# Rows scattered by expert and running rank in attention, and a second mixture that starts on full blocks inside the end of attention

## The chip, the cores and the metric

One NeuronCore of a Trainium2 chip runs the whole program. The metric is the device time of one execution in microseconds, as a median of several runs. Beside it one execution is recorded by the hardware profiler; all rows shown are of that one.

## The reference

Sixteen sequences of 256 tokens, 256 wide (N = 4096 tokens). What matters here is the last layer; the stages before it are a first mixture of experts, a product-key layer (its stage is called the peer stage) and a recurrence.

```
h = layernorm(x); q, k, v = h @ w_qkv + b_qkv
x = x + softmax(q k^T / 4) v @ w_o + b_o                    # 16 heads
h = layernorm(x) * ln2_g + ln2_b
topv, topi = top_k(h @ gate_w + gate_b, 2); gw = softmax(topv)   # 8 experts
out_e = relu(h @ W1[e] + b1[e]) @ W2[e] + b2[e]             # 256 -> 1024 -> 256
return x + sum over the two chosen e of gw * out_e
```

## The kernel before

Five engines (TensorE, VectorE, ScalarE, GpSimd, SyncE) each run a list of instructions in the order in which the code writes them, and meet through semaphores. Nothing is reordered: an instruction that waits holds all behind it on its engine. `e.wait_ge(s["x"], n)` is such a wait.

**Peer stage.** 32 blocks of 128 tokens. SyncE stores x1 (`x1_sync`), writes the recurrence's input to a scratch in HBM and reads it back (`xw_sync`); it has nothing else to do there.

**Attention.** `attn_tensor`, `attn_vector`, `attn_scalar`, `attn_gpsimd` and `attn_sync` walk over slots t; a sequence q starts every four slots, and `at(t, o)` gives the q whose step of offset o falls in slot t. A unit i (64 in all, four a sequence) is eight heads' halves: `rows_tensor` (scores for the maxima), `cols_tensor` (transposed scores), `exp_scalar`, `values_tensor`. By sequence there are, in this order: `xh_gpsimd` (slot 4q-2: the normed rows, line 1430), `h1_tensor` (slot 4q, line 1441), projections, the maxima (`max_sync`, whose rows go by DMA), `back_tensor`/`back_vector` (transposing the heads back and dividing), `oT`, `wo_tensor` (L1636), `res_vector` (the residual, L1645), `norm2_vector` (statistics and a first guess of 1/sigma), `norm2_gpsimd` (adds x to the output buffer, L1675; twelve small Newton operations, L1380 to L1386; `norm2_end`, L1668), `h2_tensor`, `gate_tensor` (L1703) and `gate_vector` (L1709), `top_vector` (two best experts), `weight_scalar`/`weight_vector`, and `rows_store_sync`, which stores the normed rows and their two weights at the token's place in `xn_scratch`. The loop ends with slot 66; the tail (units 58 to 63, sequences 13 to 15) is written out by hand.

**Routing.** When all sequences are through, `route_vector` and `route_tensor` count the 8192 choices per expert by matmuls with a triangle and with ones, give each choice a slot in blocks of 128 of one expert, and invert that table (which token stands in slot s) with one-hot tables and 64 f16 matmuls (`invert_vector`, `invert_tensor`, line 181). All engines then meet in `stage_end`.

**Second mixture.** NBK = 71 blocks of 128 slots, enough for any split. GpSimd gathers a block's rows by an indirect DMA (`xs_load_gpsimd`, helper line 206) and adds the block's result to the output by another that accumulates (`y_add_gpsimd`, L2387). TensorE runs, for n = 0 to 71: `head_tensor(n+1)` (two transposes), `up_tensor(n)` (32 matmuls, L2253), `down_tensor(n-1)` (16 matmuls, L2268). VectorE copies the expert's W1 (`w1_vector`, L2326, 128x2048) and evacuates half of the hidden units, ScalarE copies W2 and evacuates the other half. The PSUM banks alternate between two blocks.

## Time and profile before

| | |
|---|---|
| median of 3 runs | 2958.82 us (2957.26 to 2960.76) |
| the profiled execution | 2952.11 us |
| its span, first to last recorded instruction | 2950.3 us |
| mean granted TensorE clock | 0.987 of full |
| first mixture and peer stage | up to some 1976 us |
| attention | to 2396 us |
| routing | 2396 to 2421 us |
| second mixture | 2421 to 2950 us |

PE is TensorE's matmuls, PEld its weight loads, DVE VectorE, ACT ScalarE, POOL GpSimd, SP SyncE (SPq its DMA issues). L12 is line 12 of the kernel; the line can be that of a helper, so gathers of all stages show as L206. A bracket at a row's end is the idle time before it and what ended it.

### The profile page before, as it was taken

The numbers are of one execution on the slowest core, as the hardware profiler recorded it, in microseconds if no ns is written. First come the engines' busy times: TensorE is split into PE (matmuls) and PEld (weight loads), VectorE is DVE, ScalarE is ACT, GpSimd is POOL, SyncE is SP. The second block draws the span as 40 slices with busy tenths as digits, with TensorE's granted clock in tenths as the row PEclk, the third lists the DMA queues.
The fourth block names the chain that finished last, engine by engine and source line by source line (L and its number), as shares of the span: only waits on it lengthen the run. The fifth ranks groups of instructions, "written<-read, shape, count | busy, mean of one in ns | idle before, by whom it ended". The sixth has DMA issues, their size and how long they took to land.

```text
span 2950.3 us, 72654 instructions
## 1 busy us (share of the span) xinstructions
PE 2836.3 (96%) x28558; PEld 2186.6 (74%) x28558; DVE 1917.1 (65%) x6569; ACT 1213.0 (41%) x2720; POOL 496.9 (17%) x642
## 2 busy tenths in 40 slices
PE   8999879999999999999999999988999969999998
PEld 4795468777777777777777777655666659999998
DVE  4563487777777777777777777556777754444443
ACT  2332232433333333333343433245555535555554
POOL 0554400000000000000000000022444323333333
PEclk9999989999999999999999999999999979999999
DMA  3552400101010101010101010111222142222222
GB/s 142 170 164 79 148 1 23 34 23 34 24 34 23 34 23 34 23 34 23 34 23 34 23 34 23 43 46 41 70 77 63 49 133 35 39 37 37 37 37 33
DMA packets 94322, 148.90 MB, mean 50 GB/s; under 512 B 20048, under 2 KB 76240, under 8 KB 90896
## 3 DMA queue, kind: packets, MB, share of 16 engines
q1 hardware_dynamic: 73728, 107.83, 11.1%
q0 software_dynamic: 20112, 36.40, 6.1%
q8 instruction: 228, 3.74, 0.5%
q14 instruction: 110, 0.90, 0.1%
q10 hardware_dynamic: 144, 0.03, 0.0%
HBM read 95.93 MB, written 48.27 MB: 49 GB/s over the span
## 4 chain that ended last, share of the span: by engine, by line
PE 86%; DVE 5%; DMA 4%; ACT 2%; issue 2%; SPq 0%; POOL 0%; POOLq 0%; DVEq 0%; ACTq 0%
PE ps L1008 16%; PE ps L827 15%; PE ps L2253 9%; PE ps L1077 8%; PE ps L2268 8%; PE ps L1044 4%; PE ps L989 4%; DMA arena<-ys_scratch,arena 3%; PE ps L420 2%; PE ps L431 2%; PE ps L857 2%; PE ps L858 2%; PE ps L1564 2%; PE ps L1515 1%; PE ps L1585 1%
## 5 line engine op out<-in xcount | busy, mean ns | idle before, releaser
L827 PEld LDWEIGHTS ps<-arena 128*128 128x128 f32 x4096 | 537.5, 193 | 29.0 <-issue 2.9
L1008 PE MATMUL ps<-arena 128*128 128x256 f32 x2048 | 549.8, 392 | 1.9 <-DVE arena L1018 1.0
L827 PE MATMUL ps<-arena 128*128 128x128 f32 x4096 | 540.0, 276 | 0.9 <-ACT arena L835 0.9
L1008 PEld LDWEIGHTS ps<-arena 128*128 128x128 f32 x2048 | 354.2, 190 | 162.9 <-issue 132.9
L835 ACT ACTIVATE arena<-ps 128x256 f32<-128x256 f32 x512 | 195.3, 382 | 543.2 <-PE ps L827 542.6
L1077 PE MATMUL ps<-arena 128*16 128x256 f32 x4096 | 270.6, 382 | 8.2 <-DVE arena L1107 7.4
L1805 POOL MEMSET arena<- 128x3072 f32 x1 | 2.7, 2657 | 1566.3 <-PE ps L1008 1566.3
L2253 PE MATMUL ps<-arena 128*128 128x128 f32 x2272 | 265.4, 275 | 0.0
L2253 PEld LDWEIGHTS ps<-arena 128*128 128x128 f32 x2272 | 259.4, 192 | 0.2
L2268 PE MATMUL ps<-arena 128*128 128x256 f32 x1136 | 256.8, 379 | 0.0
L1098 DVE SCALAR_TENSOR_TENSOR arena<-arena 128x128 f32<-128x128 f32 x256 | 73.8, 288 | 280.4 <-ACT arena L1089 280.4
L2268 PEld LDWEIGHTS ps<-arena 128*128 128x128 f32 x1136 | 210.5, 190 | 25.7
L1089 ACT ACTIVATE arena<-ps 128x256 f32<-128x256 f32 x256 | 98.1, 383 | 305.3 <-PE ps L1077 305.3
L1526 DVE TENSOR_REDUCE arena<-ps 128x2 f32<-128x512 f32 (+1 forms) x192 | 155.8, 863 | 50.8 <-PE ps L1515 50.6
L1077 PEld LDWEIGHTS ps<-arena 128*16 128x16 f32 x4096 | 94.5, 96 | 125.3 <-issue 63.4
L2354 DVE TENSOR_TENSOR arena<-ps,arena 128x256 f32<-128x256 f32 x71 | 30.1, 425 | 224.8 <-PE ps L2268 224.8
L2387 POOL DMA_INDIRECT out<-arena x71 | 114.6, 1614 | 316.5 <-DVE arena L2360 313.5
L972 DVE TENSOR_TENSOR arena<-arena 128x2048 f16<-128x2048 f16 x128 | 155.4, 1214 | 0.0
L998 DVE TENSOR_TENSOR arena<-arena,ps 128x1024 f32<-128x1024 f32 x128 | 151.6, 1184 | 0.0
L989 PE MATMUL ps<-arena 64*128 64x32 f16 x8192 | 123.9, 174 | 13.8 <-DVE arena L977 13.8
L2297 ACT ACTIVATE arena<-arena 128x2048 f32 x71 | 135.5, 1908 | 3.4 <-PE ps L2268 2.9
L989 PEld LDWEIGHTS ps<-arena 64*128 64x128 f16 x8192 | 111.3, 93 | 30.5 <-DVE arena L977 15.4
(288 smaller groups left out, 4626.7 us busy)
## 6 DMA issues: line engine op xcount, KB each, us to landing
xw_scratch<-arena SPq DMA_DIRECT2D x32, 512.0 KB, 2.7
arena<-xw_scratch SPq DMA_DIRECT2D x256, 64.0 KB, 2.7
arena<-in_W SPq DMA_DIRECT2D x16, 1024.0 KB, 5.3
ys_scratch<-arena SPq DMA_DIRECT2D x71, 128.0 KB
xn_scratch<-arena SPq DMA_DIRECT2D x32, 129.0 KB, 3.2
arena<-in_xT SPq DMA_DIRECT2D x8, 512.0 KB, 8.4
arena<-in_kinT SPq DMA_DIRECT2D x8, 512.0 KB
arena<-in_xtb SPq DMA_DIRECT2D x32, 128.0 KB, 2.3
```

What stands on the lines that cost most here:

```text
L827: m = e.matmul(bank(b)[:, 128 * i:128 * i + 128], kin[:, k, 2 * jp + i, :], xcT[:, k, 128 * blk:128 * blk + 128], start=(k == 0), stop=(k ...
L835: e.activation(G[blk % 2][:, 2 * jp:2 * jp + 2, :], bank(2 + jp % 2)[:, 0:256].rearrange("p (a b) -> p a b", a=2), ACT.Gelu).then_inc(s["G ...
L972: e.tensor_tensor(X[b], iota_pairs(128), pairs(r_[:, 0, t0:t0 + 16], 128), ALU.is_equal)
L989: m = e.matmul(bank(4 + half)[:, 32 * q:32 * q + 32], X[b][p0:p0 + 64, q // 2, :, q % 2], Y12[b][p0:p0 + 64, i, q // 2, :, q % 2], start=( ...
L998: e.tensor_tensor(gv, gv, bank(4, 2).rearrange("p (g t j) -> p g j t", g=2, j=32), ALU.mult).then_inc(s["A"], 1)
L1008: m = e.matmul(bank(7)[:, 0:256], G[blk % 2][:, j, :], kout[:, j, :], start=(j == 0), stop=(j == 31))
L1044: m = e.matmul(bank(h), xcT[:, k, 128 * blk:128 * blk + 128], Wx[:, k, 512 * h:512 * h + 512], start=(k == 0), stop=(k == 1))
L1077: m = e.matmul(gate_ps[32 * g:32 * g + 16], hT_, Wh[:, k, 256 * g:256 * g + 256], start=False, stop=(k == 1), skip_group_check=True)
L1526: e.tensor_reduce(mx[q % 2][:, :, c, 4 * v + j:4 * v + j + n].rearrange("p b j -> p j b"), bank(b + j, n).rearrange("p (j b k) -> p j b k" ...
L2253: m = e.matmul(bank(b)[:, 128 * (f % 4):128 * (f % 4) + 128], Wb1[i][:, k, 128 * f:128 * f + 128], hb[i][:, k], start=(k == 0), stop=(k == 1))
L2268: m = e.matmul(bank(6 + i)[:, 0:256], hid[i][:, f], Wb2[i][:, f], start=(f == 0), stop=(f == 7))
L2297: e.activation(Wb2[n % 2].rearrange("p a b -> p (a b)").unsqueeze(1), Wr2[:, bass.ds(r, 1)], ACT.Copy).then_inc(s["a_w2"], 1)
```

## The change

**Rows.** Each expert gets an area of PITCH = 4224 rows in `xn_scratch`, which now holds 1152 x 31 rows of 260 words: 256 values, two weights, the token's number and its first expert. In the peer stage SyncE fills all of it with pad rows, 1152 at a time. After each sequence's `top_vector`, `choice_vector` makes one-hot rows of the two choices; one period later `before_tensor` counts, with a triangle and ones in f16, the equal choices ahead of each token, and `rank_vector` adds the running count per expert and has four lists of 128 row numbers. `rows_out_gpsimd` writes the rows of the sequence there with four indirect DMAs, in place of SyncE's two plain ones. The inversion and the barrier are gone.

**Blocks.** After sequence 7, `first_table_vector` (slots 57 and 58) lists the blocks that are full by then; they serve for the first FIRST_N = 24 of the 71. `last_table_vector`, in three parts behind blocks 7 to 9, lists the rest. Both tables give an expert and 128 consecutive rows per block. NBK stays 71.

**Order.** The second mixture's blocks 0 to 4 are interleaved by hand with the end of attention for sequences 13 to 15, on all engines. Blocks below RAMP = 6 have one set of PSUM banks (4, 5, 6, 7), so that `head`, `up` and `down` of a block wait for their evacuations in the block before. Buffers move: the gathered rows lie on rows of `hall` that have been written out, `Wb1` and `Wb2` on keys, queries and values, `b2r` on `OT` (loaded after `back` of sequence 15). The norm of sequence 15 goes from VectorE to GpSimd. W1 and W2 are loaded at other slots.

```diff
@@ peer_sync
                 xw_sync(e, blk)
+                if blk < 31:
+                    e.dma_start(xnd[FILL * blk:FILL * blk + FILL], I["padrow"]).then_inc(s["nrow"], 16)
@@ new functions
+        def route_init_vector(e):
+            d = s["qd"]
+            e.tensor_scalar(run[0], iota8, float(PITCH), None, ALU.mult).then_inc(d, 1)
+            e.memset(c1, 0.0).then_inc(d, 1)
+            e.tensor_copy(tri16, tri).then_inc(d, 1)
+            e.tensor_copy(one16, ones).then_inc(d, 1)
+            e.wait_ge(s["nrow"], 528)
+            e.tensor_copy(hall_u[:, :, 258], ids).then_inc(d, 1)
+        def choice_vector(e, q):
...
+            e.tensor_copy(hall[:, m, 259], ii8[:, m, 0]).then_inc(d, 1)
+            e.tensor_copy(r_i.rearrange("p (a b) -> p a b", b=2), ii8[:, m, 0:2]).then_inc(d, 1)
...
+            e.tensor_tensor(r_o, r_i.unsqueeze(2).to_broadcast([128, 4, 8]), iota8.unsqueeze(1).to_broadcast([128, 4, 8]),
+                            ALU.is_equal).then_inc(d, 1)
...
+            e.tensor_tensor(r_s, o[:, :, 0], o[:, :, 1], ALU.add).then_inc(d, 1)
+        def before_tensor(e, q, b):
+            r = bank(b)
+            e.wait_ge(s["qd"], seq(q) + 4)
+            e.matmul(r[:, 16:32], tri16, flat(r_s), start=True, stop=False)
+            e.matmul(r[:, 24:32], one16, r_s[:, 0], start=False, stop=True)
+            e.matmul(r[:, 32:40], one16, r_s[:, 0], start=True, stop=False)
+            e.matmul(r[:, 32:40], one16, r_s[:, 1], start=False, stop=True).then_inc(s["as_cum"], 1)
+        def rank_vector(e, q, b):
...
+            e.tensor_copy(slots[:, 4 * q:4 * q + 4], r_f).then_inc(d, 1)
+        def rows_out_gpsimd(e, q):
+            if q:
+                e.wait_ge(s["rsc"], 64 * q)
+            e.wait_ge(s["po_xn"], q + 1)
             e.wait_ge(s["po_dd"], 4 * q + 4)
+            e.wait_ge(s["qd"], seq(q) + 9)
+            for j in range(2):
+                for k in range(2):
+                    c = 4 * q + 2 * j + k
+                    e.indirect_dma_start(xnd, bass.IndirectOffsetOnAxis(ap=slots[:, c:c + 1], axis=0), hall[:, 2 * q + j], None
+                                         ).then_inc(s["rsc"], 16)
@@ attn_tensor, attn_vector
                     gate_tensor(e, q)
+                    if q:
+                        before_tensor(e, q - 1, 6)
...
                 for q in at(t, 24):
                     gate_vector(e, q)
+                    if q:
+                        rank_vector(e, q - 1, 6)
...
                     top_vector(e, q)
+                    choice_vector(e, q)
+                if t in (57, 58):
+                    first_table_vector(e, t - 57)
@@ attn_gpsimd
                 for q in at(t, -2):
                     if q:
                         xh_gpsimd(e, q)
-            for q in (13, 14, 15):
-                norm2_gpsimd(e, q)
+                for q in at(t, 29):
+                    rows_out_gpsimd(e, q)
@@ moe2_tensor
             head_tensor(e, 0)
-            for n in range(NBK + 1):
+            e.wait_ge(s["ot"], 63)
+            values_tensor(e, 63, 0)
+            head_tensor(e, 1)
+            up_tensor(e, 0)
...
+            gate_tensor(e, 13, 3)
+            before_tensor(e, 12, 3)
...
+            back_tensor(e, 15, 0)
+            head_tensor(e, 2)
+            up_tensor(e, 1)
...
+            oT_tensor(e, 15, 2)
+            down_tensor(e, 0)
+            wo_tensor(e, 15, 0)
...
+            h2_tensor(e, 14, 1)
+            head_tensor(e, 3)
+            up_tensor(e, 2)
...
+            gate_tensor(e, 14, 3)
+            before_tensor(e, 13, 3)
+            down_tensor(e, 1)
...
+            h2_tensor(e, 15, 2)
+            head_tensor(e, 4)
+            up_tensor(e, 3)
...
+            for n in range(5, NBK + 1):
                 if n + 1 < NBK:
                     head_tensor(e, n + 1)
                 if n < NBK:
                     up_tensor(e, n)
-                if n:
-                    down_tensor(e, n - 1)
+                down_tensor(e, n - 1)
@@ moe2_gpsimd
-            e.wait_ge(s["iv"], 39)
-            for n in range(NX):
-                xs_load_gpsimd(e, n)
+            norm2_gpsimd(e, 13)
+            xs_load_gpsimd(e, 0)
+            xs_load_gpsimd(e, 1)
+            rows_out_gpsimd(e, 10)
+            rows_out_gpsimd(e, 11)
+            norm2_gpsimd(e, 14)
+            xs_load_gpsimd(e, 2)
+            xs_load_gpsimd(e, 3)
+            rows_out_gpsimd(e, 12)
             for n in range(NBK):
                 y_add_gpsimd(e, n)
                 if n + NX < NBK:
                     xs_load_gpsimd(e, n + NX)
+                if n == 0:
+                    norm2_gpsimd(e, 15)
+                if n < 3:
+                    rows_out_gpsimd(e, 13 + n)
@@ gate2_vector
+            if n >= NX:
+                e.wait_ge(s["acc"], 16 * (n - NX + 1))
```

## Rows read from the trace of the kernel before

**Rows 1.** The page, part 1: busy us (share of the span) and instructions

```profile
PE 2836.3 (96%) x28558; PEld 2186.6 (74%) x28558; DVE 1917.1 (65%) x6569; ACT 1213.0 (41%) x2720; POOL 496.9 (17%) x642
```

**Rows 2.** Windows: each engine's busy us, then granted clock, DMA share, GB/s

```profile
2396.00:2421.00 25.00, 9.54 (x69) 7.68 (x69) 21.88 (x60) 5.14 (x5) 0.00 (x0) 0.57 0.21 66
...
2421.00:2427.00 6.00, 5.28 (x19) 4.20 (x19) 2.89 (x6) 0.67 (x2) 4.53 (x4) 0.77 0.17 44
...
2460.00:2560.00 100.00, 100.00 (x695) 93.76 (x694) 47.62 (x140) 52.68 (x98) 36.11 (x28) 1.00 0.24 38
```

**Rows 3.** The chain that ended last, from 2377 to 2442 us: start, us, what

```profile
2377.07 1.07 PE ps L1585 x16
...
2417.81 1.23 PE ps L181 x16
...
2427.39 3.70 PE ps L2253 x32
...
2431.31 3.57 PE ps L2253 x32
...
2438.56 3.57 PE ps L2253 x32
```

**Rows 4.** The same chain at the span's end

```profile
2934.74 3.47 PE ps L2268 x16
```

**Rows 5.** Timeline, first gathers and last add: start, us, engine, line [idle before]

```profile
2421.56 1.66 POOL L206 DMA_INDIRECT arena<-xn_scratch,arena  x1 [33.84 <-DVEq L73]
...
2421.87 1.23 DVE L2326 COPY arena<-arena 128x2048 f32 x1 [1.09 <-issue]
...
2425.05 0.16 DVE L2345 TENSOR_TENSOR arena<-arena 128x1 f32<-128x1 f32 x1 [0.66 <-DMA arena<-xn_scratch,arena]
...
2425.44 0.95 POOL L206 DMA_INDIRECT arena<-xn_scratch,arena  x1 [0.30 <-issue]
...
2944.09 1.55 POOL L2387 DMA_INDIRECT out<-arena  x1 [3.04 <-DMA out<-arena]
```

**Rows 6.** Timeline of one attention period, from `h1` on

```profile
2243.57 0.66 PE L1441 MATMUL ps<-arena 128*128 128x128 f32 x4
...
2245.06 0.17 DVE L1709 TENSOR_TENSOR arena<-ps,arena 128x16 f32<-128x16 f32 x1
...
2246.89 0.76 DVE L1645 TENSOR_TENSOR arena<-ps,arena 128x256 f32<-128x256 f32 x2 [1.65 <-PE ps L1636]
...
2247.39 1.32 POOL L1675 TENSOR_TENSOR arena<-arena 128x256 f32<-128x256 f32 x2 [7.13 <-DVE arena L1645]
...
2254.70 0.19 POOL L1380 TENSOR_TENSOR arena<-arena 128x2 f32<-128x2 f32 x1 [5.99 <-DVE arena L1376]
...
2258.05 2.43 POOL L1668 TENSOR_SCALAR arena<-arena 128x256 f32<-128x256 f32 x2
...
2260.46 2.42 POOL L1430 TENSOR_SCALAR arena<-arena 128x256 f32<-128x256 f32 x2
```

**Rows 7.** Timeline, start of the next period

```profile
2266.72 2.42 DVE L1526 TENSOR_REDUCE arena<-ps 128x2 f32<-128x512 f32 x3 [0.94 <-PE ps L1515]
...
2267.60 0.66 PE L1441 MATMUL ps<-arena 128*128 128x128 f32 x4
...
2268.09 0.96 PE L1703 MATMUL ps<-arena 128*128 128x8 f32 x8
...
2268.90 1.97 PE L1636 MATMUL ps<-arena 128*128 128x256 f32 x8
```

**Rows 8.** Timeline, VectorE at the start of attention

```profile
1985.70 0.98 DVE L1487 TENSOR_SCALAR arena<-ps,arena 128x256 f32<-128x256 f32 x2
```

**Rows 9.** Timeline of SyncE's issues in one block of the peer stage

```profile
1213.30 3.82 SPq L1066 DMA_DIRECT2D arena<-xw_scratch  x8
...
1241.02 0.34 SPq L1023 DMA_DIRECT2D x_scratch<-arena  x1
```

**Rows 10.** DMA issues of the page: KB each, us to landing

```profile
xn_scratch<-in_zrow SPq DMA_DIRECT2D x1, 129.0 KB, 2.8
```

More of the change, by code:

```diff
@@ L1327, in build @@
         VA = take(3, 2, 16, 32)
-        PT = [take(4, 512) for _ in range(2)]
-        assert arena.at <= WORDS - 10240
+        r_i, r_o, r_s, r_r, r_p, r_f = take(4), take(4, 8), take(2, 8, dt=f16), take(2, 8), take(4, 8), take(4)
+        t_u, t_n, t_m, end1, end2, t_w = take(8, dt=u32), take(8), take(8), take(8), take(8), take(8)
+        t_b, t_i, t_d = take(1), take(8), take(8)
+        t_r, t_r1 = take(72), take(32)
+        gt = [take(2) for _ in range(2)]
+        yi, ids = take(4, dt=u32), take(32)
+        assert arena.at <= WORDS - 16384
+        bo, bv = take(256), take(256)
+        xh, h1T = take(2, 256), take(2, 256)
+        wqkv = take(2, 768)
+        t_c1 = take(32, 8)
+        assert arena.at <= WORDS - 16384 + 4096
+        t_c2 = take_at(hall_at + 24 * ROWW, 72, 8)
+        keep, arena.at = arena.at, route_at
+        slots, b1 = take(64, dt=u32), take(8, 8)
+        eid1, row1, ef1 = take(32, dt=u32), take(32, dt=u32), take(32)
+        eid2, row2, ef2 = take(72, dt=u32), take(72, dt=u32), take(72)
+        run, c1 = [take(8) for _ in range(2)], take(9)
+        bb1 = [take(8) for _ in range(2)]
+        assert arena.at <= base
+        arena.at = iot_at
+        tri16, one16 = take(128, dt=f16), take(128, dt=f16)
+        arena.at = keep
         ROW = (16, 0)
@@ L1751, in early_sync @@
+        def early_sync(e, v, x):
+            if v == 0:
+                if x < 4:
+                    e.wait_ge(s["n1_cp"], 32)
+                elif x < 6:
+                    e.wait_ge(s["vm"], 58)
+                else:
+                    e.wait_ge(s["rsc"], 64 * (4 if x == 6 else 8))
+            elif x < 2:
+                for name, n in (("p_mm", 64), ("p_vm", 32), ("p_vv", 32), ("p_tr", 16), ("p_hb", 16), ("iv", 34)):
+                    e.wait_ge(s[name], n)
             w, name, done = ((Wr1, "W1", "ew1"), (Wr2, "W2", "ew2"))[v]
@@ L2098, in attn_vector @@
             gate_vector(e, 11, 3)
+            rank_vector(e, 10, 3)
             top_vector(e, 11)
+            choice_vector(e, 11)
             back_vector(e, 14, 1)
             gate_vector(e, 12, 3)
+            rank_vector(e, 11, 3)
             weight_vector(e, 11)
@@ L2285, in head_scalar @@
             e.wait_ge(s["a_tr"], NBK + n + 1)
+            if n == 0:
+                e.wait_ge(s["rsc"], 64 * 10)
             if n >= 2:
@@ L2312, in moe2_scalar @@
             head_scalar(e, 0)
-            e.wait_ge(s["ew2"], 128)
-            for n in range(NBK):
+            values_scalar(e, 63, 0)
+            h2_scalar(e, 13, 2)
+            head_scalar(e, 1)
+            w2_scalar(e, 0)
+            weight_scalar(e, 12)
+            up_scalar(e, 0)
+            head_scalar(e, 2)
+            w2_scalar(e, 1)
+            up_scalar(e, 1)
+            h2_scalar(e, 14, 1)
+            head_scalar(e, 3)
+            w2_scalar(e, 2)
+            weight_scalar(e, 13)
+            up_scalar(e, 2)
+            h2_scalar(e, 15, 2)
+            head_scalar(e, 4)
+            w2_scalar(e, 3)
+            weight_scalar(e, 14)
+            up_scalar(e, 3)
+            head_scalar(e, 5)
+            w2_scalar(e, 4)
+            weight_scalar(e, 15)
+            up_scalar(e, 4)
+            for n in range(5, NBK):
                 if n + 1 < NBK:
@@ L2362, in moe2_vector @@
         def moe2_vector(e):
-            e.wait_ge(s["ew1"], 128)
-            e.wait_ge(s["eb"], 32)
-            e.wait_ge(s["qd"], 26)
-            e.wait_ge(s["iv"], 39)
             w1_vector(e, 0)
-            for n in range(NBK + 1):
+            res_vector(e, 14, 1)
+            norm2_vector(e, 14)
+            w1_vector(e, 1)
+            gate2_vector(e, 0)
+            up_vector(e, 0)
+            gate_vector(e, 13, 3)
+            rank_vector(e, 12, 3)
+            back_vector(e, 15, 0)
@@ new lines, in moe2_vector @@
+            weight_vector(e, 12)
+            top_vector(e, 13)
+            choice_vector(e, 13)
+            w1_vector(e, 2)
+            gate2_vector(e, 1)
+            up_vector(e, 1)
+            oT_vector(e, 15, 2)
+            down_vector(e, 0)
+            w1_vector(e, 3)
+            res_vector(e, 15, 0)
+            norm2_vector(e, 15)
+            gate2_vector(e, 2)
+            up_vector(e, 2)
+            gate_vector(e, 14, 3)
+            rank_vector(e, 13, 3)
+            weight_vector(e, 13)
@@ new lines, in moe2_vector @@
+            top_vector(e, 14)
+            choice_vector(e, 14)
+            down_vector(e, 1)
+            w1_vector(e, 4)
+            gate2_vector(e, 3)
+            up_vector(e, 3)
+            gate_vector(e, 15, 3)
+            rank_vector(e, 14, 3)
+            weight_vector(e, 14)
+            top_vector(e, 15)
+            choice_vector(e, 15)
+            down_vector(e, 2)
+            w1_vector(e, 5)
+            gate2_vector(e, 4)
+            weight_vector(e, 15)
+            up_vector(e, 4)
@@ L2369, in moe2_vector @@
+            down_vector(e, 3)
+            rank_vector(e, 15, 3)
+            for n in range(5, NBK + 1):
                 if n + 1 < NBK:
```

473 lines of the change are left out of this document (290 added, 183 removed).

## The prediction

> **What bounds the kernel now.** I read four views in this order. The page says that TensorE is busy for 96% of the span [rows 1], so only stages in which it is not can give much. The busy times by stage show one hole: steady work of the second mixture has PE busy 100 of 100 us at clock 1.00, but from 2396 to 2421 us PE is busy 9.5 of 25 us at a granted clock of 0.57 [rows 2]. The chain that ended last shows what lies there: the last values matmuls of attention start at 2377.07, the first expert block's up matmuls at 2427.39 [rows 3], and between them stand the end of attention, VectorE's counting and the inversion on one-hot tables (its last matmuls, L181, at 2417.81), and the first gather. From 2431.31 a block passes every 7.25 us (to 2438.56), and `down` of block 69 ends at 2934.74 + 3.47 = 2938.21 [rows 3, 4]. Last, the timeline of one attention period of 24.03 us, 2243.57 to 2267.60 [rows 6, 7]: PE works nearly through, and GpSimd's work stands between VectorE's guess of the rstd and the next sequence's `h1_tensor`.
>
> **What the change takes away.** Inversion and barrier go, and block 0 waits only for its own gather. PE can take `head_tensor(0)` right behind the values of unit 62, at 2377.0. If nothing stalled, it would then have to do: values of unit 63, 1.1; blocks 0 to 69 as before, 2427.39 to 2938.21 = 510.8; and what is left of attention, which before lay in the hole: three gates, `wo`, one `back`, one `oT`, two `h2` and four `before_tensor`. Start to start, four transposes take 0.49 and a gate 0.81 (`h1` at 2267.60, gate at 2268.09, `wo` at 2268.90, which itself takes 1.97 [rows 7]); with five groups of four transposes that is 2.4 + 2.0 + 2.5 = 6.9 us. `before_tensor` is in no row. Sixteen f16 matmuls of 144 columns take 1.23 us [rows 3], 0.077 each, so four narrower ones are at most 0.31 (and nothing, if they hide in the wait for a neighbour); having fewer columns they are nearer 0.25, which I take, 1.0 for four. `down` of block 69 would end at 2377.0 + 0.2 for the head + 1.1 + 510.8 + 7.9 = 2897.0: a gain of 41.2 us.
>
> **What comes back in the ramp.** The new order is strict on each engine, and GpSimd's is the longest. Prices: a gather holds it 0.95 us and the next begins 0.30 later; what it brings can be read 1.8 us after its instruction ends (2421.56 + 1.66 = 2423.22, and VectorE, waiting for it, starts at 2425.05) [rows 5]. `norm2_gpsimd` is 1.32 + 3.35 (from 2254.70 to 2258.05) + 2.42 = 7.1 us [rows 6]. An adding scatter is 1.55 + 0.30 [rows 5]. A plain scatter is in no row. Lower bound: the gather's 0.95, which also moves each row once; upper bound: the adding scatter's 1.55, which shares the direction but must also read the old row. I take 0.95, since it has the same count of reads and writes, and keep 1.55 for the range. One `rows_out_gpsimd` is then 4 x 1.25 = 5.0 us (7.4 at the upper bound).
>
> GpSimd is free at 2367 (end of the norm of sequence 13; its first part is as before). Two gathers to 2369.6, `rows_out(10)` to 2374.6, then `rows_out(11)` waits for the landing of those rows (some 1.9) and runs 2376.5 to 2381.5, norm of 14 to 2388.6, gather 2 to 2389.9, landed 2391.7. PE meanwhile does block 0's up, gate 13 and `back` 15 and is through at 2384.4; next in its queue is `head_tensor(2)`, so it stands for 7.3 us, and `up(1)` and `down(0)` behind it. The same accounting, carried on over the four queues, gives: `down(0)` ends 2401.3, and only then the first add, gather 4 and the norm of 15 (2412.6, PE waits 0.6 for it); gathers 5, 6 and 7 come behind `rows_out` 13, 14 and 15 and make PE wait 1.0, 0.7 and 4.1 us. In sum 13.7 us of standing. Two of these gaps are long. In the profile the clock sat at 0.57 while PE had little to do and was 0.77 on average from 2421 to 2427, when PE was busy again [rows 2]: about 2.8 of 6 us at half. Each long gap thus costs up to 1.8, together 3.6. Ramp: 41.2 - 13.7 - 3.6 = 23.9. The weight copies (L2326) collide with some scatters: the gather beside such a copy held GpSimd 1.66 instead of 0.95 [rows 5], and two such meetings cost 1.4. So 22.5.
>
> The Trainium skill ("SBUF — State Buffer", in the section on its two separate sides) says why: a VectorE copy in a two-port mode locks GpSimd out, so that it cannot write descriptors, until the copy ends. The trace agrees (1.66 against 0.95). By that rule every meeting costs up to a whole copy, 1.23, and five of them, one in each `rows_out` of the ramp, would make it 20 instead of 22.5; I keep to two, since no row shows how often they meet.
>
> **What attention pays.** (a) `route_init_vector`: five small operations at some 0.17 to 0.2 each before VectorE's projections; its q1 ends at 1985.70 + 0.98 = 1986.68 [rows 8], just when the scores begin, so all 0.8 us shows. (b) `choice_vector` (four operations, 0.8) goes into 0.94 us of idle time before the maxima [rows 7], and `rank_vector` (six, 1.2) behind the gate, before the `wo` sum, where VectorE idles 1.65 [rows 6]: nothing; without that cover 2.0 a period. (c) `before_tensor`, 0.25 on PE each period. (d) `rows_out_gpsimd(q)` stands in GpSimd's queue between the norm's end and `xh_gpsimd`. That now runs 2260.46 to 2262.88, and `h1_tensor` needs it at 2267.60 [rows 6, 7]: 4.7 us, less a hand-over of 0.1. Five us do not fit. The lateness isn't made up, since `h1`, `wo`, the residual, the statistics, the guess and GpSimd's norm hang on each other in a ring: a period becomes 24.03 + 0.25 + (5.0 - 4.6) = 24.68. `rows_out` 0 to 7 have an `xh` behind them: 8 x 0.65 = 5.2. Two more periods pay 0.25 each. (e) `first_table_vector`, some 3.5 us of VectorE in two busy slots, mostly in idle time: 1. Together 7.5.
>
> (f) The fill: 31 transfers of 1.2 MB from SyncE, each behind the loads of a block. SyncE's issues end at 1217.12 and its next stands at 1241.02 [rows 9]; 129 KB from HBM to HBM landed in 2.8 us [rows 10], so 1.2 MB takes between 2.8 (if latency is all) and 26 us (if it scales), against 24 free, and what comes next there, a store of x1, has a further 18 us. Nothing. Without this cover a late `xw` load stops the recurrence. (g) `last_table_vector`, up to 3.3 us a block in blocks 7 to 9: VectorE is busy 48 of 100 us there [rows 2], 3.8 idle per block: nothing. (h) The gate's two more small operations and the wait for `acc`: the same cover. (i) W1 and W2 loads and b2: earlier than their readers by several us. (j) The end behind the last `down` is unchanged.
>
> **Sum.** 22.5 - 7.5 = 15 us faster: the profiled execution took 2952.1 with a span of 2950.3; its span would be 2935.3. The median of the runs shown, 2958.8, is 6.7 above the profiled one; I carry the difference over: 2943.8. About 0.2% (6 us) is what a measurement can tell from no change.
>
> **Rivals.** *Scatters at the adding scatter's price* (1.55). One mechanism, GpSimd's queue, in both places: a period is 24.03 + 0.25 + 7.4 - 4.6 = 27.1, so attention pays 8 x 3.05 + 2.3 = 26.7; the ramp's gain falls to about 11.8. Slower by 14.9: 2973.7. For: it is the only row that writes to HBM by index. Against: the add needs one more read per row, and 1.55 / 0.95 is close to three accesses over two. It decides from 1.25 us a scatter on (each 0.1 us costs 3.2 in attention and 1.8 in the ramp). *The queue does not bind in attention* (period rises by 0.25 only, the slack in PE's waits absorbs the rest): 3.2 more, 2940.6, and with the clock staying up in the ramp 2937. For: PE waits twice in a period; against: those waits lie behind PE's own work. *Scatters of 1.1 to 1.3*, by collisions or a partly dearer write: from 7.5 faster to 2.5 slower, 2951 to 2961. *No change in fact*, because the ramp is wholly GpSimd-bound and gives back all: would need another 14 us of gaps; only with the dear scatter.
>
> **Chances.** Forecast 0.52, attention not bound 0.13, middling scatter 0.15, dear scatter 0.18, the fill disturbing the peer stage 0.02. Faster by over 0.2%: 0.48 of the first, the second, 0.03 of the third: 0.64; same 0.14; slower 0.22. The range runs from 2937 (not bound, clock up) to 2974 (the dear case). The likeliest case alone: 2939 to 2950.
>
> **What the new profile would show.** Time of a plain scatter on GpSimd (0.95 or 1.55); attention's period from the fifteenth or so of its slots on, 24.7 against 24.03, with PE waiting for L1430's line before `h1`; PE's wait of about 7 us before `head(2)`, then 4 before `head(7)`, with a lower clock behind them; steady blocks at 7.25 us; `down(69)` ending near 2923 us; the peer stage unchanged at 48.7 us a block. Wrong if the scatter is dear, if the waits on landed scatters (`rsc`) are longer than 1.9 us, or if the fill shifts the peer blocks.

## The result, and the profile after it

The changed kernel took 2968.97 us in the median of six runs (2966.86 to 2976.0), the kernel before 2956.83 in six beside them: ratio 1.0046, 95% interval 1.0034 to 1.0059. The forecast was 2943.8, so not only the size but the sign is wrong. On another chip, as the experiments will show, the same kernel took 2942.9 and was faster. The profiled execution took 2976.0 with a span of 2974.2; it lies 7.0 over its median, that of before 4.7 under its own, so the two traces differ by 24 us where the medians differ by 12.

The chain that ended last, at the span's end in the changed kernel, against [rows 4]:

```profile
2956.21 3.57 PE ps L2397 x32
2959.78 3.47 PE ps L2414 x16
```

The last down matmuls on it (block 69's) end at 2963.25 instead of 2938.21, 25.0 us later. Two starts divide this into three parts, that of `norm2_gpsimd(0)` and that of `norm2_gpsimd(12)`. Timelines of the kernel before and of the changed one:

```profile
2056.07 1.32 POOL L1675 TENSOR_TENSOR arena<-arena 128x256 f32<-128x256 f32 x2 [22.01 <-DVE arena L1645]
2343.42 1.32 POOL L1675 TENSOR_TENSOR arena<-arena 128x256 f32<-128x256 f32 x2 [10.87 <-DVE arena L1645]
...
2061.29 1.41 POOL L1698 TENSOR_TENSOR arena<-arena 128x256 f32<-128x256 f32 x2 [23.80 <-DVE arena L1674]
2379.01 1.41 POOL L1698 TENSOR_TENSOR arena<-arena 128x256 f32<-128x256 f32 x2 [8.47 <-DVE arena L1674]
```

The first part is 2061.29 against 2056.07, 5.2 later, before any row is scattered. In between attention takes 317.72 instead of 287.35, 30.4 us more. From there to the end the changed kernel needs 584.2 instead of 594.8: the ramp does give back, but 10.6 us. 5.2 + 30.4 - 10.6 = 25.0.

The 5.2 us is not the change's. Windows from 1990 to 2060 us, before and then after (the granted clock is the third number from the end):

```profile
1990.00:2060.00 70.00, 57.72 (x607) 40.65 (x608) 48.35 (x84) 34.08 (x60) 15.92 (x31) 0.98 0.13 42
1990.00:2060.00 70.00, 58.10 (x534) 40.98 (x535) 43.52 (x76) 31.43 (x55) 14.04 (x24) 0.85 0.06 21
```

The clock was 0.98 in the one and 0.85 in the other. The same changed kernel once more (after_again below) has 0.98 there and starts `norm2_gpsimd(0)` at 2055.28; before_quads, which has the old kernel's code up to there, has 0.85 and starts it at 2062.22.

The price of a plain scatter, which no row of before showed, was forecast at 0.95 us on GpSimd. All instructions of its line:

```profile
L1819 POOL DMA_INDIRECT xn_scratch<-arena x64: 956/968/1952, 2145.8 to 2484.4; - x64
```

The median is 0.968. So the scatter is not dear, and the loss in attention is something else. One `rows_out_gpsimd` with what surrounds it, from the timeline of the changed kernel (start, us, engine, line, idle time before it and what ended that):

```profile
2284.10 1.07 PE L1614 MATMUL ps<-arena 128*32 128x256 f32 x16
...
2284.76 0.97 POOL L1819 DMA_INDIRECT xn_scratch<-arena  x1 [0.30 <-issue]
...
2285.54 0.60 PE L1652 MATMUL ps<-arena 128*128 128x128 f32 x4
...
2285.98 0.60 PE L1708 MATMUL ps<-arena 128*128 128x128 f32 x4
...
2286.95 0.38 ACT L1623 ACTIVATE arena<-ps 128x256 f32<-128x256 f32 x1 [2.41 <-remote]
2287.30 0.96 POOL L1819 DMA_INDIRECT xn_scratch<-arena  x1 [0.30 <-issue]
...
2288.31 2.43 POOL L1459 TENSOR_SCALAR arena<-arena 128x256 f32<-128x256 f32 x2
...
2289.15 0.69 DVE L1659 COPY arena<-ps 128x512 f32<-128x512 f32 x1 [2.07 <-remote]
2289.21 1.02 ACT L1717 ACTIVATE arena<-ps,arena 128x256 f32<-128x256 f32 x2 [0.93 <-remote]
...
2289.99 1.15 PE L1593 MATMUL ps<-arena 32*128 32x256 f32 x16 [2.55 <-DVE arena L1659]
```

This is the reading on which the rest of the study hangs. ScalarE's L1623 needs the values matmuls L1614. These end at 2284.10 + 1.07 = 2285.17, and L1623 starts at 2286.95, 1.8 us later, though ScalarE stood idle. VectorE's L1659 needs the transposes L1652, over at 2286.14, and starts at 2289.15: 3.0 us later, the last 2.07 of them idle (it was busy with L1555 up to 2287.08). The view says "remote" for both. On one core that can be no other core: it is what it prints when the signal came long after every instruction that gives it had ended. TensorE's next scores (L1593) then wait 2.55 us for L1659. A signal the other way is not late: L1659 ends at 2289.84 and L1593 starts 0.15 later. L1659 and L1717 start 0.06 us apart, while the two groups that they wait for start 0.44 apart on TensorE. So it looks as if TensorE had done both and its signals had been held and let go together; the ends of matmuls are modelled, so this is argued and not shown. I call it late completions. In none of the twenty traces of this study is a wait of TensorE itself listed as "remote".

Summed over 2130 to 2370 us (waiting engine and line, for whom, us in total, times, longest):

```profile
ACT arena L1623 <- remote: 22.2, 9, 3.2
DVE arena L1555 <- PE ps L1544: 20.5, 15, 1.8
PE ps L1593 <- DVE arena L1659: 19.2, 8, 2.5
...
DVE arena L1659 <- remote: 15.3, 8, 2.1
```

No wait of `h1_tensor` (L1470) for `xh_gpsimd` (L1459) is in that list, the one that I had forecast. The periods, from one start of `norm2_gpsimd` to the next, are 23.14, 24.02 and 24.12 us as long as no row is scattered, and then 28.36, 26.69, 28.13, 25.99, 28.39, 26.72, 28.14 and 26.77, against 24.03 before. Two things are in them: in the four of over 28 us the granted clock is 0.94, in the other four it is 1.00. So late completions alone make a period some 2 to 3 us longer, and the periods with the lower clock are another 1.4 to 2.4 longer.

### The profile page after: what moved, and what is told of

It is laid out like the page before. It is cut to its first block, busy times and chain, and to the rows that moved or that the text cites. A ratio compares the mean times of both kernels' runs of the same rounds, so it can differ in the third digit from the quotient of the medians.

```text
span 2974.2 us, 73021 instructions
## 1 busy us (share of the span) xinstructions
PE 2841.4 (96%) x28538; PEld 2190.0 (74%) x28538; DVE 1947.1 (65%) x6849; ACT 1207.8 (41%) x2716; POOL 574.4 (19%) x720
## 3 DMA queue, kind: packets, MB, share of 16 engines
q8 instruction: 228, 3.74, 0.5%
## 4 chain that ended last, share of the span: by engine, by line
PE 87%; DVE 5%; ACT 2%; issue 2%; DMA 1%; another core or an unknown queue 1%; POOL 1%; SPq 0%; POOLq 0%; DVEq 0%; ACTq 0%
PE ps L1010 16%; PE ps L829 15%; PE ps L1079 8%; PE ps L2397 8%; PE ps L2414 8%; PE ps L1046 4%; PE ps L991 4%; PE ps L422 2%; PE ps L433 2%; PE ps L1593 2%; PE ps L859 2%; PE ps L860 2%; PE ps L268 2%; PE ps L269 2%; PE ps L1544 2%
## 5 line engine op out<-in xcount | busy, mean ns | idle before, releaser
L2397 PE MATMUL ps<-arena 128*128 128x128 f32 x2272 | 270.6, 278 | 0.6 <-DVE arena L2599 0.6
L2397 PEld LDWEIGHTS ps<-arena 128*128 128x128 f32 x2272 | 264.9, 195 | 0.9 <-issue 0.8
L1555 DVE TENSOR_REDUCE arena<-ps 128x2 f32<-128x512 f32 (+1 forms) x192 | 155.7, 862 | 54.5 <-PE ps L1544 53.5
```

Source lines behind the costliest of these rows:

```text
L1555: e.tensor_reduce(mx[q % 2][:, :, c, 4 * v + j:4 * v + j + n].rearrange("p b j -> p j b"), bank(b + j, n).rearrange("p (j b k) -> p j b k" ...
L2397: m = e.matmul(bank(up_bank(n) + f // 4)[:, 128 * (f % 4):128 * (f % 4) + 128], Wb1[i][:, k, 128 * f:128 * f + 128], hb[i][:, k], start=(k ...
```

## The experiments

The kernels were run in five groups, each on one chip beside the kernel before; the five chips, A to E, are different ones. Which chip gave the result above is not known; it may be one of them. "Period" is from one start of `norm2_gpsimd` to the next while rows of sequences 0 to 6 go out, read from the profile (the periods of sequences 7 and 8 are not in the range; the first of them also holds `first_table_vector`). Two forms take more in these two than the range says: pair_here 26.6 to 26.8 on both chips, quad_moved 29.3 and 27.9.

| kernel | chip | period, us | median, us | ratio to before, 95% interval |
|---|---|---|---|---|
| att_none | A | 24.13 | 2941.4 | 0.9948 (0.9925 to 0.9972) |
| att_busy | A | 24.13 | 2937.9 | 0.9930 (0.9908 to 0.9953) |
| att_gather | A | 24.61 to 24.75 | 2950.4 | 0.9981 (0.9968 to 0.9994) |
| att_pairs | A | 24.13 | 2939.0 | 0.9942 (0.9923 to 0.9961) |
| quad_moved | B | 26.75 to 27.22 | 2973.6 | 1.0053 (1.0036 to 1.0070) |
| pair_here | B | 24.55 to 24.95 | 2951.0 | 0.9983 (0.9973 to 0.9992) |
| ramp_spread | B | 25.59 to 25.91 | 2944.4 | 0.9960 (0.9947 to 0.9973) |
| before_quads | B | 26.3 to 28.3 | 2989.5 | 1.0104 (1.0087 to 1.0121) |
| after_again | C | 26.65 to 28.36 | 2969.8 | 1.0053 (1.0034 to 1.0072) |
| att_pairs_again | C | 25.57 to 25.81 | 2956.3 | 0.9997 (0.9985 to 1.0008) |
| before_quads_1k | C | 25.8 to 28.5 | 2980.9 | 1.0077 (1.0052 to 1.0102) |
| pair_here_again | C | 24.54 to 25.16 | 2953.8 | 0.9982 (0.9970 to 0.9993) |
| after_third | D | 24.66 to 24.78 | 2942.9 | 0.9955 (0.9943 to 0.9966) |
| att_gather_again | D | 24.61 to 24.77 | 2949.1 | 0.9985 (0.9971 to 0.9998) |
| att_half | D | 24.12 | 2936.2 | 0.9945 (0.9925 to 0.9966) |
| att_singles | D | 24.12 to 24.14 | 2940.6 | 0.9951 (0.9936 to 0.9967) |
| mixed | E | see below | 2946.3, one run | |
| best | E | 24.13 | 2923.4 | 0.9892 (0.9864 to 0.9919) |

**Chip A.** Three kernels put something else in the place of the scatters of sequences 0 to 9:

```diff
                     c = 4 * q + 2 * j + k
+                    if q < 10:
+                        h = hx[:, 2 * q + j, k:k + 1]
+                        e.tensor_scalar(h, h, 1.0, None, ALU.mult).then_inc(s["fk"], 1)
+                        continue
```

That is att_none. att_busy has `h = hx[:, 2 * q + k]`, all 256 columns. att_gather has for sequences 1 to 9:

```diff
+                        e.indirect_dma_start(hall[:, 2 * (q - k) + j], None, xnd,
+                                             bass.IndirectOffsetOnAxis(ap=slots[:, c:c + 1], axis=0)).then_inc(s["rsc"], 16)
```

att_pairs takes `rows_out_gpsimd(q)` from slot 29 and puts its first half behind `xh_gpsimd` (slot 30) and its second behind the two adds of `norm2_gpsimd(q + 4)`.

> Left out: the 40 scatters of sequences 0 to 9; each is replaced by a one-column operation on GpSimd, so those rows of the list keep the filler. All else of the changed kernel stays. Every theory that puts the loss on the scatters expects the attention period back at 24.1 to 24.3 us (24.03 before, 27.3 on average in the changed kernel) and some 28 to 30 us less than the changed kernel: 2939 to 2943. If choice, rank or before_tensor cost the time, the period stays over 25.5 and the total over 2955. If the ramp alone then differs, the total shows what the ramp is worth by itself.

24.13 and 2941.4. So choice, rank and `before_tensor` cost 0.10 us a period together. I also took it that all the rest is the scatters'; but the changed kernel itself was not run on chip A, which turned out to be free of late completions, so that is shown only by before_quads below.

> Left out: the 40 scatters of sequences 0 to 9; each is replaced by a GpSimd operation on 256 columns, 1.21 us, so GpSimd is held for some 5 us at the same place but no DMA is written. Theory Q (the prediction's step: GpSimd's queue delays xh and h1): nearly the period of the changed kernel, 27 us, total about 2968. Theory H (TensorE's completions are told late while GpSimd issues indirect DMAs): no late completions, period 24.1 to 24.8, total 2939 to 2948.

24.13, but this run tells less than meant. The timeline of att_busy shows the four operations (L1827) at 0.86 us each, not 1.21:

```profile
2260.10 3.43 POOL L1827 TENSOR_SCALAR arena<-arena 128x256 f32<-128x256 f32 x4
2263.52 2.44 POOL L1459 TENSOR_SCALAR arena<-arena 128x256 f32<-128x256 f32 x2
```

3.43 us fit into the 4.6 that `xh_gpsimd` can spare by the forecast's own count, so the queue was not put to the test.

> Changed: the scatters of sequences 1 to 9 become gathers by the same indices (HBM to SBUF, into rows already sent), same count, place and bytes; so those rows of the list keep the filler. Theory H, issuing side: period 26.5 to 28.5 as in the changed kernel, TensorE's completions late by 1.5 to 3 us as there, total about 2968. Theory L (the landing of scattered rows, reads of SBUF or writes of HBM, delays TensorE): period 24.1 to 24.8 and total 2940 to 2950.

24.61 to 24.75, no "remote" wait; I took it for a proof that only writing brings late completions. Its total can't be compared: the edit makes a load of W1 wait for one more sequence, and that holds SyncE's queue at the end of attention (periods 27.7 and 21.2 there).

> Same work, but the four scatters of sequences 0 to 8 stand in two pairs: two behind xh_gpsimd, two behind the adds of the next norm, each where GpSimd otherwise waits some 5 us for VectorE. Theory Q: nothing of the 5 us is left on the ring, period 24.1 to 24.3, total about 2942. Theory H: the completions are late at other places, and less (pairs of indirect DMAs in the second mixture delay none); period between 24.3 and 26.5, total 2945 to 2962. If only the number of scatters counts, the total stays at 2968.

24.13, no late completion, 2939.0 with the work complete.

**Chip B.** quad_moved: all four scatters to slot 30, behind `xh_gpsimd`. pair_here: the first half stays in slot 29, the second goes behind `xh_gpsimd`. ramp_spread is att_pairs and, in `moe2_gpsimd`:

```diff
             rows_out_gpsimd(e, 10)
-            rows_out_gpsimd(e, 11)
             norm2_gpsimd(e, 14)
             xs_load_gpsimd(e, 2)
             xs_load_gpsimd(e, 3)
-            rows_out_gpsimd(e, 12)
+            rows_out_gpsimd(e, 11)
...
-                if n < 3:
-                    rows_out_gpsimd(e, 13 + n)
+                if 1 <= n < 9:
+                    rows_out_gpsimd(e, 12 + (n - 1) // 2, ((n - 1) % 2,))
```

before_quads is the kernel before with four scatters of `wqkv[:, j, 0:258]` into a tensor of its own added behind `norm2_gpsimd(q + 3)`, by indices 32 rows apart.

> Same work: the four scatters of sequences 0 to 8 stay one behind the other, but stand behind xh_gpsimd instead of ahead of it, where GpSimd otherwise waits for VectorE. Theory B (a burst of four scatters is what makes TensorE's completions late, wherever it stands): late completions of 1.5 to 3 us again, period 25.5 to 28. Theory P (only the place counts, what TensorE or the queues do there): none late, period 24.1 to 24.3, total 2939 to 2943 as with the pairs.

> Same work: two of the four scatters stay at the place of the changed kernel, ahead of xh_gpsimd, the other two stand behind xh_gpsimd (sequences 0 to 8). Theory B (burst of four): none late, 24.1 to 24.3, total about 2940. Theory P (the place): the first pair alone makes TensorE's completions late by about half as much, period 25 to 26.5, total 2948 to 2960.

> The pairs of att_pairs, and in the ramp the order of GpSimd's work changed: norm2 of sequence 14 and gathers 2 and 3 ahead of rows_out(11), and rows_out 12 to 15, which only blocks from 24 on read, in pairs, one in each of the blocks 1 to 8. If GpSimd's queue is what made TensorE stand 21.7 us in the ramp of att_pairs (10.3 before head(2), 3.5 before h2 of 15, 1.2, 1.3, 5.4), that falls by 10 to 15 us: total 2924 to 2931, ratio to before 0.989 to 0.992. If the landing of the gathers or the loads of W1 and W2 hold the ramp, the total stays over 2936.

> The kernel before, with four scatters of 128 rows of 1032 B added for each of the sequences 0 to 9 behind norm2_gpsimd of the sequence three later, as in the changed kernel, from a constant tile to a part of HBM that nobody reads; the work of the kernel is complete. The ring for GpSimd's descriptors has its 16 KB here and 8 KB in the changed kernel. Theory R (the halved ring is what makes it dear): no late completions, period 24.0 to 24.3, total within 4 us of before. Theory H (back-to-back scatters at that place, whatever the ring): late completions and a period of 26.5 to 28.5, total 2980 to 2990.

Late completions are there in all four, also in pair_here, where they cost less than either theory had (24.7). before_quads has the old kernel's routing and its 16 KB ring and goes to 26.3 to 28.3 all the same: the ring's size is out, and so is all else of the change but the scatters. Added alone to the old kernel they make a period 2 to 4 us longer. quad_moved stays at 27: `xh_gpsimd` is ahead of the scatters there, so GpSimd's queue is not the cause on this chip. But ramp_spread has the attention of att_pairs, operation for operation, and a period of 25.6 instead of 24.13. Either the programs or the chips differ. Its total, 2944.4, lies over the 2936 that was to mean that landings or loads hold the ramp. That doesn't follow here: late completions lengthen attention to 300.6 us (290.2 in att_pairs), and they stand in the ramp too, up to 7.4 us in one wait. The run best below tries the same order without them.

**Chip C.** The changed kernel, att_pairs and pair_here once more, unaltered, and before_quads with 256 words a row at a pitch of 256.

> The changed kernel once more, as the yardstick on this chip: 2966 to 2976, period 26.7 to 28.4 with late completions. If it comes out at 2940 to 2950 without them, the lateness belongs to a chip or a loading of the program and not to the kernel.

> The kernel att_pairs once more. In its first run no completion of TensorE was late (period 24.13, 2939.0); ramp_spread, with the same code in attention, had them (25.6). If the state belongs to the kernel: 2936 to 2942 again. If it belongs to the chip or to the loading: 25.6 a period, 2948 to 2956.

> before_quads with rows of 1024 B at a pitch of 1024 B instead of 1032 B at 1032 B. Theory A (rows that don't end on a boundary of HBM's, a short packet behind each, make the scatter dear for others): none late, period 24.0 to 24.3. Theory H (any four plain scatters at that place): 26.5 to 28.2 as in before_quads.

> The kernel pair_here once more beside the others: as in its first run, 24.7 a period and late completions, if the state belongs to the kernel; at 24.13 if it belongs to the chip or the loading and this one is free of it.

att_pairs came out at 25.6 and 2956.3 (ten runs, 2951.5 to 2962.6; the six on chip A were 2936.0 to 2947.6). One and the same kernel has no late completions on A and has them on C. That also takes away what I had read from att_gather and att_pairs, whose chip was free of them. With rows of 1024 B completions are late as well, so the odd length isn't it.

**Chip D.** The changed kernel a third time, att_gather again, att_half (for sequences 0 to 9, `if k: continue`, with the counts of `rsc` to match) and att_singles (one scatter behind `norm2_gpsimd`, one between the halves of `xh_gpsimd`, one behind it, one behind the adds).

> The changed kernel once more, as the yardstick on the chip of this call: period 26.7 to 28.4 with late completions as on two chips so far; 24.1 to 24.7 if this chip is free of it, and then the three others show nothing on this question.

> The kernel att_gather once more (scatters of sequences 1 to 9 turned into gathers, those rows keep the filler). If only writing to HBM by index makes completions late: none late and 24.6 a period as in its first run, where after_third has 27. If any indirect DMA does, and its first run was on a chip free of it: late, and 26.5 to 28.

> Left out: the second scatter of each row for sequences 0 to 9, so two scatters a sequence instead of four, at the place of the changed kernel; the rows of the second choice keep the filler. If lateness follows the count: 25.3 to 26 a period, half of the loss. If a burst of four is needed: 24.13. If the place is what counts and one is enough: over 26.5.

> Same work: the four scatters of sequences 0 to 8 stand singly, one behind norm2_gpsimd, one between the two halves of xh_gpsimd, one behind it, one behind the adds of the next norm, 1.4 us or more apart. If closeness makes completions late: none, 24.13 to 24.3 a period, total 2938 to 2944 whatever the chip. If each scatter costs by itself: 25.5 to 27, total 2950 to 2966.

The changed kernel took 2942.9 us (2938.2 to 2946.9, eight runs), ratio 0.9955. The forecast had been 2943.8. With no late completion about, attention looks as forecast; timeline of after_third:

```profile
2264.04 2.43 POOL L1691 TENSOR_SCALAR arena<-arena 128x256 f32<-128x256 f32 x2
2266.63 1.08 POOL L1819 DMA_INDIRECT xn_scratch<-arena  x1 [0.16 <-issue]
...
2270.56 0.96 POOL L1819 DMA_INDIRECT xn_scratch<-arena  x1 [0.30 <-issue]
2271.57 2.45 POOL L1459 TENSOR_SCALAR arena<-arena 128x256 f32<-128x256 f32 x2
...
2274.16 0.63 PE L1470 MATMUL ps<-arena 128*128 128x128 f32 x4 [0.50 <-POOL arena L1459]
```

From 2266.47 to 2271.57 the rows go out, 5.1 us, and `h1_tensor` waits 0.50 us for the `xh` behind them: the period is 24.67, forecast 24.68. att_half and att_singles, whose GpSimd holds `xh` up for 2.6 us and less, stand at 24.12: so it is the queue, and here the forecast's bound of 4.6 us is tested from both sides. Four gathers (24.61) cost what four scatters cost. On late completions the four kernels of this chip say nothing, whatever their form.

**Chip E.** best is att_singles with the ramp of ramp_spread. mixed was to hold several forms in one program:

```diff
+                    if q in (6, 7) and k:
+                        continue
```

and the gather of att_gather for sequences 3 to 5.

> One program with several forms of rows_out: four scatters for sequences 0 to 2 and 8 to 9, four gathers by the same indices in their place for 3 to 5, two scatters (the first choice alone) for 6 and 7; the rows that are not sent keep the filler. On a chip without late completions: 24.7, 24.6, 24.1, 24.7 a period. On one with them: scatters by four 26.7 to 28.4; gathers 24.6 if only writing brings lateness, 26.5 to 28 if reading does too; scatters by two 25.3 to 26 if it follows the count, 24.1 if a burst of four is needed.

> Complete work: att_singles with the ramp's order of ramp_spread. On a chip without late completions, attention 24.12 a period and a ramp some 4 us shorter than that of att_singles: 2933 to 2939, ratio 0.992 to 0.994. On a chip with them: if singles keep clear of them, 24.2 to 24.8 and 2938 to 2945; if each single scatter still costs, 25.5 and 2945 to 2952.

Chip E was free of late completions too: scatters by four 24.67 to 24.76, gathers 24.61 and 24.62 (sequences 3 and 4). The periods of sequence 5 and of the halved 6 and 7 (25.74, 29.39, 25.51) say nothing: a W1 load that this edit makes wait longer held SyncE's queue (22.2 us, by the list of SyncE's waits), and the last holds `first_table_vector`. So the question that mixed was made for stays open. best took 2923.4 us, some 10 less than the least that was expected: the new order made the ramp 17.6 us shorter, not some 4.

## A mark that stood in the trace of before

With chips known to differ, the first stage of the first mixture is worth a look: nine gathers of `x_tb` stand back to back on GpSimd there (83.5 to 94.8 us in the kernel before). Waits of the kernel before from 84 to 110 us:

```profile
DVE arena L466 <- remote: 3.6, 1, 3.6
...
ACT arena L446 <- remote: 2.5, 1, 2.5
POOL arena L206 <- remote: 1.7, 1, 1.7
ACT arena L439 <- remote: 1.1, 1, 1.1
```

And its timeline there:

```profile
93.88 0.95 POOL L206 DMA_INDIRECT arena<-in_xtb,arena  x1 [0.30 <-issue]
...
94.08 1.06 PE L420 MATMUL ps<-arena 128*128 128x128 f32 x8
94.85 0.38 ACT L446 ACTIVATE arena<-ps 128x256 f32<-128x256 f32 x1 [2.47 <-remote]
```

The same stretch in after_third has no such line; VectorE's copy waits for TensorE by name:

```profile
DVE arena L468 <- PE ps L433: 5.6, 8, 1.1
```

The list has a "remote" wait in that stretch in nine of ten profiles: those of the kernel before and of the result, and the eight from chips B and C but for ramp_spread. It has none in the ten from A, D and E. So the late completions were in the kernel before, as single waits of 1.1 to 3.6 us that were never followed up, and gathers bring them too. What those waits cost in all, no run tells. What each scatter or gather does to them isn't simple: on the chip of the result, from 2520 to 2900 us, where an adding scatter and a gather of each block stand one behind the other, no "remote" wait is listed.

## Why the prediction was wrong

**The scatter's price** was right: 0.968 against 0.95; one `rows_out` is 5.1 us against 5.0. The dear-scatter rival, though its 2973.7 lies nearest to what was measured, has the wrong cause.

**Step (d), "a period becomes 24.03 + 0.25 + (5.0 - 4.6) = 24.68".** This is where the prediction failed. On the chip of the result a period is 26.0 to 28.4. The mechanism forecast is real and of its size (24.67 on chip D, 24.67 to 24.76 on E), but on the chip of the result another one covers it: TensorE's completions come 1.8 to 3 us late at `values_scalar`, `oT_vector` and `h2_scalar` while rows go out. None of my rivals had it. It costs 2969 to 2970 less 2942.9, some 26.5 us, by the medians of the same kernel with it (the result, chip C) and without it (chip D); before, beside them, had 2956.8, 2959.2 and 2956.3. In the traces of the result and of chip D, attention between the two starts above takes 317.7 against 293.3 us, and what follows 587.7 against 585.4. Part of it goes with the clock, 0.94 in four of eight periods; the forecast had no clock term in attention. The sentence "wrong if the scatter is dear, if the waits on landed scatters are longer, or if the fill shifts the peer blocks" named three things. On the chip of the result none of them happened (a wait on landed rows was 1.75 there). On chip D the second did, 2.8 instead of 1.9, which is about 1 us in the ramp and nothing beside the 26.5.

**The small terms of attention.** `before_tensor` with choice and rank: 0.10 a period, forecast 0.25; `first_table_vector`: one period of 25.8 in att_none, 1.7 more, forecast 1.0; `route_init_vector`: 0.6, forecast 0.8 (from the first `h1_tensor` to `norm2_gpsimd(0)` it is 77.2 us in att_pairs, att_pairs_again, ramp_spread and att_singles against 76.6 before, all at a granted clock of 0.98 from 1990 to 2060). On chip D attention from `norm2_gpsimd(0)` to `(12)` took 293.3 us against 287.35: 6.0 more, forecast 6.7 without route_init; with it 6.6 against 7.5.

**The ramp, forecast at 22.5.** Without late completions it gives 12.8 (from `norm2_gpsimd(12)` to the end of block 70's down: 585.4 us in after_third against 598.2 before; 13.4 in att_pairs, 12.7 in att_singles). TensorE's long waits in the timeline of after_third, with two `up_tensor` (L2397) at different clocks:

```profile
2403.21 0.47 PE L2378 MATMUL ps<-arena 128*128 128x128 f32 x1 [9.52 <-DMA arena<-xn_scratch,arena]
...
2403.69 6.41 PE L2397 MATMUL ps<-arena 128*128 128x128 f32 x32
...
2416.22 3.74 PE L2397 MATMUL ps<-arena 128*128 128x128 f32 x32
...
2427.89 0.63 PE L1708 MATMUL ps<-arena 128*128 128x128 f32 x4 [3.49 <-POOL arena L1691]
...
2437.93 0.33 PE L2378 MATMUL ps<-arena 128*128 128x128 f32 x1 [1.17 <-DMA arena<-xn_scratch,arena]
...
2446.92 0.33 PE L2378 MATMUL ps<-arena 128*128 128x128 f32 x1 [1.44 <-DMA arena<-xn_scratch,arena]
...
2459.77 0.47 PE L2378 MATMUL ps<-arena 128*128 128x128 f32 x1 [5.38 <-DMA arena<-xn_scratch,arena]
```

They sum to 21.0 where I had 13.7 and, for collisions, 1.4: 9.5 before `head(2)` (forecast 7.3), 3.5 before `h2` of sequence 15 (0.6), then 1.2, 1.4 and 5.4 (1.0, 0.7, 4.1). The clock is the second part. TensorE was idle from 2393.7 to 2403.2; from 2396 to 2408 the granted clock is 0.50, and `up(1)` takes 6.41 us where it takes 3.74 at 1.00. With the second long wait, 5.4 us, the low clock costs some 5.0 us, where I had 3.6 (and my 1.8 a gap did not come out of its own row: 2.8 us at half are 1.4). Together these two are 7.3 of the 9.7 us that were missed; the other 2.4 I can't place. All the waits are on GpSimd's chain, as said; what was too short is my account of it. GpSimd's part of the timeline up to `head(2)`, with one copy of VectorE:

```profile
2382.67 0.97 POOL L1819 DMA_INDIRECT xn_scratch<-arena  x1 [0.30 <-issue]
2386.42 0.97 POOL L1819 DMA_INDIRECT xn_scratch<-arena  x1 [2.78 <-DMA xn_scratch<-arena]
2387.70 1.79 POOL L1819 DMA_INDIRECT xn_scratch<-arena  x1 [0.30 <-issue]
...
2396.82 3.35 POOL L1691 TENSOR_SCALAR arena<-arena 128x256 f32<-128x256 f32 x2
2397.48 1.23 DVE L2558 COPY arena<-arena 128x2048 f32 x1 [0.67 <-issue]
2400.33 1.06 POOL L208 DMA_INDIRECT arena<-xn_scratch,arena  x1 [0.16 <-issue]
```

The wait for landed rows is 2.8 (I had 1.9), a scatter takes 1.79 beside VectorE's weight copies as forecast, and `norm2_end`, two plain operations, takes 3.35 instead of 2.43, which I had not thought of: that weight copy of VectorE (L2558, 2397.48 to 2398.71) lies inside it. In the ramp six operations of GpSimd are stretched so, the scatters to 1.79, 1.55 and 1.96, a gather to 2.02, `norm2_end` to 3.35 and 3.17, together 5.1 us over their usual length; I had allowed 1.4. The Trainium skill ("SBUF — State Buffer", on its two separate sides) has the port pair that both share locked for a whole instruction by whichever of the two starts first, while the other waits. The trace agrees with the length (0.6 to 1.05 us more, beside copies of 1.23 to 1.43), but not with who waits: `norm2_end` started 0.66 us before the copy, the copy took its usual 1.23, and GpSimd was the one held up. By the skill's rule the forecast had named five meetings as the other possibility, and that was nearer, though its figure is off: five copies of 1.23 are 6.2 and leave 17.7, not 20. That GpSimd's queue held the ramp is shown by best, which differs from att_singles by the order of this queue alone (they ran on chips E and D, both without late completions): from `norm2_gpsimd(12)` to the end of block 70's down it takes 567.9 us, 17.6 less than att_singles (and than after_third), with 5.66 left before its third head.

**The rest, and luck.** The steady blocks pass every 7.25 us, the peer stage and the table in blocks 7 to 9 cost nothing, as forecast. By the traces attention's 6.0 less the ramp's 12.8 makes 6.8 faster on chip D, while the medians there say 13.3. Much of the gap is the clock at the start of attention, which differs from one execution to the next of any kernel. After_third's profile has 0.86 there and takes 83.4 us from the first `h1_tensor` to `norm2_gpsimd(0)`, where 0.98 gives 77.2; the profile of before has 0.98 and lies 4.7 under its median. Of before's 23 executions on chip D, the ten with a mean clock of 0.987 or more have a median of 2952.0 us, the twelve at 0.985 or less 2958.0; six of the changed kernel's eight have 0.988 or more, with a median of 2942.0. At a like clock, then, the gain is some 10 us and not 13.3; whether the changed kernel meets the lower clock less often by its own doing is not shown. Stages before attention vary as well (the first `h1_tensor` stands between 1974.4 and 1980.7 us in the twenty traces). The close hit of 2942.9 by 2943.8 is therefore partly luck: the ramp missed by 9.7 us and attention by 0.9 the other way, and what lies outside both made up for the rest.

## What to carry to other kernels

A wait that this profile puts down to "remote" on one core is a signal that came late; it deserves to be followed up even where it is 2 us long, since a change can put the same thing onto the critical path in every period. Keep indirect DMAs apart from each other: in GpSimd's idle time it costs nothing where they do no harm (24.13 against 24.67 us a period), and on the chips with late completions pairs cost 0.5 to 1.5 us a period where bursts of four cost 2 to 4. (Singles were not run on such a chip.) Look at the order of a queue that others wait for: the gathers and the norm ahead of rows that only later blocks read gave 17.6 us. And time a few per mille on more than one chip: the sign of this change went with the chip, 1.0046 for the result and 1.0053 on chip C, 0.9955 on chip D, each beside the kernel before.

## What the runs showed of the hardware

- On the chip of the result and on two of the five of the experiments (B and C), TensorE's completions reach ScalarE and VectorE 1.8 to 3 us after the modelled end of the matmuls while GpSimd issues indirect DMAs, and in the ramp ScalarE once idles 7.4 us for one; on A, D and E no kernel shows it. No trace lists a wait of TensorE for VectorE or ScalarE as "remote". Whether the chip itself makes it or something else that the runs of one group share, what holds the signals (the issue of the DMAs or their landing), and whether single scatters are free of it on such a chip, was not settled: the kernels that could have told ran on chips without it. The Trainium skill ("SBUF — State Buffer", on who interferes with whom) says that a DMA never contends with a compute engine; whether these traces speak against it hangs on whether the matmuls or only their signals were held, which they don't show.
- On those chips a period rises from 24.1 to 26 to 28.5 with four scatters in a row, at both places tried, with either size of the descriptor ring, and with rows of 1024, 1032 or 1040 B; to 25.6 with pairs in GpSimd's idle time, and to 24.7 (26.7 in the last two periods) with one pair behind `norm2_gpsimd` and one behind `xh_gpsimd`.
- From 1990 to 2060 us, where TensorE waits often, the granted clock is 0.98 in some executions and 0.85 or 0.86 in others, of the kernel before's code as of the changed one's, on chips with late completions and without. From the first `h1_tensor` to `norm2_gpsimd(0)` it is 76.6 to 78.3 us with the one and 83.3 to 85.3 with the other (one trace lies between, 0.93 and 81.3).
- A GpSimd tensor_scalar on 128x256 in place, with an immediate, took 0.86 us, where the one with two per-partition operands takes 1.22; the latter is stretched beside VectorE's copies as a scatter is (two took 3.35 instead of 2.43), though it had started first.
